# Recurrent mixer scan: the products of the states with r move from VectorE to GpSimd, and some small VectorE operands move to PSUM

## What is computed

```python
def step(state, rkv):
    r_t, k_t, v_t = rkv
    pred = jnp.einsum('bhij,bhj->bhi', state, k_t)
    err = pred - v_t
    state = dec * state - et * (err[..., :, None] * k_t[..., None, :])
    n = jnp.maximum(jnp.sqrt(jnp.sum(state * state, axis=(-2, -1), keepdims=True)), 1e-08)
    state = state * jnp.where(n > max_norm, max_norm / n, 1.0)
    wkv = jnp.einsum('bhij,bhj->bhi', state, r_t)
    return (state, wkv)
```

## Time and profile before

| | |
|---|---|
| median of 3 runs | 7446.54 us (7446.42 to 7454.33) |
| the profiled execution: its own time | 7440.85 us |
| the profiled execution: its span | 7439.0 us |
| stage `mixer_scan`, in the span | 230 to 1349 us |
| VectorE busy in that stage | 1063.57 of 1119 us |
| GpSimd busy in that stage | 0 us |

### The profile page before, as it was taken

How to read it: one execution, slowest core, us unless ns; L and a number is a source line. 1 busy time by engine, 2 the same in 40 slices (tenths; PEclk the granted TensorE clock), 3 DMA queues, 4 the chain that set the end, 5 groups by cost and what they waited for, 6 DMA issues and landing times. The chain is left out here.

```text
span 7439.0 us, 185174 instructions
## 1 busy us (share of the span) xinstructions
PE 6202.7 (83%) x76196; PEld 4530.6 (61%) x76196; DVE 5784.1 (78%) x10537; ACT 3453.0 (46%) x7490; POOL 3111.7 (42%) x1651
## 2 busy tenths in 40 slices
PE   6455555599996789999999999997878699999999
PEld 4445554477775655555555555554555488888888
DVE  8899999555546769999999999997565477777775
ACT  4333333233332367777777777774444311111111
POOL 1000000111110049999999999997122122222222
PEclk8767777799998899999999999998889799999999
DMA  3211111201102330211202112111111100000000
GB/s 99 62 38 47 45 40 37 67 31 41 39 14 85 119 102 20 63 39 40 56 28 57 37 40 56 40 39 40 39 50 41 74 6 7 8 7 8 8 7 6
DMA packets 385855, 312.95 MB, mean 42 GB/s; under 512 B 169443, under 2 KB 354790, under 8 KB 384646
## 3 DMA queue, kind: packets, MB, share of 16 engines
q1 hardware_dynamic: 382566, 300.75, 13.8%
q10 hardware_dynamic: 2464, 0.26, 0.0%
HBM read 193.93 MB, written 106.95 MB: 40 GB/s over the span
## 5 line engine op out<-in xcount | busy, mean ns | idle before, releaser
L1865 POOL TENSOR_TENSOR ss_ch<-ss_h,ss_c_all 128x1024 f32<-128x1024 f32 x1024 | 2401.1, 2395 | 161.3 <-DVE ss_h L1888 126.4
L1888 DVE TENSOR_TENSOR_SCAN ss_h<-ss_decay,banks 128x1024 f32<-128x1024 f32 x1024 | 2259.8, 2268 | 169.1 <-PE banks L1785 164.6
L1785 PE MATMUL banks<-ss_diag,ss_dxT 128*32 128x256 f32 x32768 | 1985.3, 383 | 85.8 <-ACT ss_diag L1835 71.7
L1785 PEld LDWEIGHTS banks<-ss_diag,ss_dxT 128*32 128x32 f32 x32768 | 1003.0, 110 | 895.6 <-DVE ss_h L1888 263.1
L1844 ACT ACTIVATE ss_decay<-ss_dt,ss_neg_a 128x510 f32<-128x510 f32 x2048 | 1359.9, 711 | 299.0 <-DVE ss_h L1888 292.8
L627 PE MATMUL banks<-ms_rprod,ident 128*128 128x128 f32 x2048 | 466.9, 400 | 509.6 <-DVE ms_rprod L713 509.6
L2190 POOL TENSOR_TENSOR pk_blockhot<-pk_onehot,pk_parts 128x2048 bf16<-128x2048 bf16 x96 | 345.4, 3626 | 1100.0 <-DVE pk_parts L2428 1100.0
L1835 ACT ACTIVATE ss_diag<-ident,ss_bT 128x128 f32<-128x128 f32 x2048 | 694.9, 387 | 224.5 <-PE banks L1785 215.1
L627 PEld LDWEIGHTS banks<-ms_rprod,ident 128*128 128x128 f32 x2048 | 431.9, 263 | 539.4 <-DVE ms_rprod L713 475.7
L1792 PE MATMUL banks<-ss_ch,ss_stacked 128*32 128x256 f32 x8192 | 639.4, 383 | 80.1 <-POOL ss_ch L1865 80.1
L1047 DVE TENSOR_REDUCE l_nmax<-banks 128x2 f32<-128x512 f32 (+1 forms) x512 | 318.2, 621 | 342.4 <-PE banks L1032 340.8
(11 more groups left out here) (295 smaller groups left out, 9593.4 us busy)
## 6 DMA issues: line engine op xcount, KB each, us to landing
ss_c_all<-keep_cn SPq DMA_DIRECT2D x512, 64.0 KB, 2.1
ss_dt<-keep_dt SPq DMA_DIRECT2D x256, 128.0 KB, 3.6
keep_v<-ms_cx_values SPq DMA_DIRECT2D x32, 512.0 KB, 2.8
l_va<-keep_v SPq DMA_DIRECT2D x32, 512.0 KB, 5.3
l_kf<-keep_k SPq DMA_DIRECT2D x32, 256.0 KB, 3.2
keep_x<-l_x SPq DMA_DIRECT2D x32, 256.0 KB, 2.2
keep_xc<-si_xc SPq DMA_DIRECT2D x16, 512.0 KB, 3.9
keep_zs<-si_zs SPq DMA_DIRECT2D x16, 512.0 KB, 4.9
```

The lines of the kernel that those rows point to most:

```text
L1785: m = T_.matmul(inp[u % 2][s * CB:(s + 1) * CB, g, :, t * P:(t + 1) * P], inputs[i % 2][0][:, g, t, u * CB:(u + 1) * CB], diag[slot][:, g, ...
L1865: G_.tensor_tensor(whole(ch[u % CHS]), whole(h[u % 4]), whole(c_all[slot]), ALU.mult).then_inc(weighed, 1)
L1888: V.tensor_tensor_scan(whole(h[u % 4]), whole(decay[u % 4]), whole(inp[u % 2]), 0.0, ALU.mult, ALU.add).then_inc(scanned, 1)
```

## The change

The change has three parts.

First, `rprod` is made by GpSimd, in a new function `gpsimd(G)`, one instruction for each of the 256 tokens. For token n it waits for the mark `multiplied` of step n + 1, which is `prod` of the next step (the instruction that reads the same state), so it starts when that one ends. Because two engines now read a state, VectorE waits in step t, ahead of the new state, until GpSimd has made the product of token t - 2, which reads the buffer that is written over. TensorE's wait for a group is adapted to a mark on every product.

Second, on VectorE the order in a step is new: `prod`, at once `raw`, and only then `inv` and `FF`.

Third, `raw` and `pred` lie in bank 7 of PSUM, and so does a copy of the decay, `dec_held`, made once. So `pred`, `fdec` and `err` have one input in PSUM and one in SBUF, where they had two in SBUF. `inv` and the reciprocal keep their one input, and their output, in SBUF. `prod`, `outer` and the new state keep two inputs in SBUF.

```diff
-    raw, pred, err = sb("raw", [P, 2 * D]), sb("pred", [P, 2 * D]), sb("err", [P, 2, D])
+    err = sb("err", [P, 2, D])
+    raw, pred, dec_held = bank[7][:, 128:128 + 2 * D], bank[7][:, 192:192 + 2 * D], bank[7][:, 256:258]
...
-                T_.wait_ge(*multiplied_r.at(q))
+                T_.wait_ge(*multiplied_r.at((q + 1) * GR - 1))
...
+        V.tensor_copy(dec_held, dec[:, :]).then_inc(*own.up())
...
-        V.wait_ge(*state.at(T - 1))
-        r_product(V, T)
...
+    def gpsimd(G):
+
+        for n in range(T):
+            if n % CH == 0:
+                G.wait_ge(*steps[n // CH % 2].at(n // CH // 2))
+            if n >= 2 * GR and n % GR == 0:
+                G.wait_ge(*summed_r.at(n // GR - 2))
+            if n < T - 1:
+                G.wait_ge(*multiplied.at(n + 1))
+            else:
+                G.wait_ge(*state.at(n))
+            G.tensor_tensor(rprod[:, n // GR % 2, n % GR, :, :].rearrange("p (e i) j -> p e i j", e=2), S_[:, (n + 1) % 2, :, :, :],
+                            rep(R_[:, n, :, :], 2, D), ALU.mult).then_inc(multiplied_r.sem, 1)
...
-        V.tensor_tensor(prod[:, :, :, :], now, rep(K_[:, t, :, :], 2, D), ALU.mult).then_inc(*own.up())
-        multiplied = own.now()
+        V.tensor_tensor(prod[:, :, :, :], now, rep(K_[:, t, :, :], 2, D), ALU.mult).then_inc(multiplied.sem, 1)
+        V.wait_ge(*multiplied.at(t))
+        V.tensor_reduce(raw, prod[:, :, :, :].rearrange("p e i j -> p (e i) j"), AX.X, ALU.add).then_inc(*own.up())
         if t:
-            r_product(V, t)
             V.wait_ge(*rooted.at(t - 1))
             V.tensor_scalar(inv[:, :], root[:, :], 1.0 / max_norm, 1.0, ALU.mult, ALU.max).then_inc(*own.up())
-        inverted = own.now()
-        V.wait_ge(*multiplied)
-        V.tensor_reduce(raw[:, :], prod[:, :, :, :].rearrange("p e i j -> p (e i) j"), AX.X, ALU.add).then_inc(*own.up())
-        if t:
-            V.wait_ge(*inverted)
+            V.wait_ge(*own.now())
             V.reciprocal(FF[:, t, :], inv[:, :]).then_inc(*own.up())
...
+        if t > 1:
+            V.wait_ge(*multiplied_r.at(t - 2))
...
+    gpsimd(nc.gpsimd)
     vector(nc.vector)
```

More of the change, by code:

```diff
@@ L574, in mixer_scan @@
     half, state, rooted = st.mark("first_head_ready"), st.mark("state"), st.mark("rooted")
-    squared, multiplied_r, summed_r, cut = st.mark("squared", 2), st.mark("r_multiplied"), st.mark("r_summed"), st.mark("r_cut")
+    squared, multiplied, multiplied_r, summed_r, cut = st.mark("squared", 2), st.mark("multiplied"), st.mark("r_multiplied"), st.mark("r_summed"), st.mark("r_cut")
     measured, spread_root, spread_ready = st.mark("measured"), st.mark("spread_root"), st.mark("spread_ready")
@@ L733, in step @@
             V.wait_ge(*state.at(t - 1))
-        V.tensor_tensor(prod[:, :, :, :], now, rep(K_[:, t, :, :], 2, D), ALU.mult).then_inc(*own.up())
-        multiplied = own.now()
+        V.tensor_tensor(prod[:, :, :, :], now, rep(K_[:, t, :, :], 2, D), ALU.mult).then_inc(multiplied.sem, 1)
+        V.wait_ge(*multiplied.at(t))
+        V.tensor_reduce(raw, prod[:, :, :, :].rearrange("p e i j -> p (e i) j"), AX.X, ALU.add).then_inc(*own.up())
         if t:
-            r_product(V, t)
             V.wait_ge(*rooted.at(t - 1))
             V.tensor_scalar(inv[:, :], root[:, :], 1.0 / max_norm, 1.0, ALU.mult, ALU.max).then_inc(*own.up())
-        inverted = own.now()
-        V.wait_ge(*multiplied)
-        V.tensor_reduce(raw[:, :], prod[:, :, :, :].rearrange("p e i j -> p (e i) j"), AX.X, ALU.add).then_inc(*own.up())
-        if t:
-            V.wait_ge(*inverted)
+            V.wait_ge(*own.now())
             V.reciprocal(FF[:, t, :], inv[:, :]).then_inc(*own.up())
         V.wait_ge(*own.now())
-        V.tensor_tensor(by_e(pred[:, :]), by_e(raw[:, :]), rep(FF[:, t, :], 2, D), ALU.mult).then_inc(*own.up())
+        V.tensor_tensor(by_e(pred), by_e(raw), rep(FF[:, t, :], 2, D), ALU.mult).then_inc(*own.up())
         predicted = own.now()
-        V.tensor_tensor(fdec[:, :], FF[:, t, :], dec[:, :], ALU.mult).then_inc(*own.up())
+        V.tensor_tensor(fdec[:, :], FF[:, t, :], dec_held, ALU.mult).then_inc(*own.up())
         V.wait_ge(*predicted)
-        V.tensor_tensor(err[:, :, :].rearrange("p e i -> p (e i)"), pred[:, :], VV[:, t, :, :].rearrange("p e i -> p (e i)"),
+        V.tensor_tensor(err[:, :, :].rearrange("p e i -> p (e i)"), pred, VV[:, t, :, :].rearrange("p e i -> p (e i)"),
                         ALU.subtract).then_inc(*own.up())
```

## The result

The changed kernel takes 7515.03 us (median of 4 runs, 7512.84 to 7516.7) against 7450.43 us for the kernel before, timed beside it: a ratio of 1.0085, 95% interval 1.0067 to 1.0102. The forecast was 7512.

What follows compares the result with a forecast made beforehand. VectorE's chain of instructions bounds the edited stage, busy 1063.57 of 1119.00 us. The step, 3.81 + 0.60 = 4.41 against 4.15 us, costs 66 us, plus 1: 7512 us; range 7350 to 7545, 8 times in 10.

Steps and rivals of the forecast that it cites:

- `prod` to `raw` 0.73: VectorE's step: `raw` starts 0.73 us after `prod`, as nothing stands between them any more.
- `raw` to `inv` 0.60: VectorE's step: `inv` starts 0.60 us after `raw`, at 1.33, with the root there since 0.88.
- from `FF` on the old distances: VectorE's step: from `FF` to the next `prod` the order and the distances between starts stay as before.
- The sum without any hold, 3.81: One step added up from starts in rows: 3.81 us, 0.34 less than 4.15, 87 us gained over 255 steps.
- rival B: `inv` of two numbers runs in the plain form, nothing is held: step 3.81, time 7361 us; chance 0.21.
- GpSimd's product: In each step it starts at 0.78 us, 0.09 after `prod` ends, and takes 1.30 (bounds 1.16 to 1.44).
- `inv` held, `FF` late by 0.60: `inv` ends with GpSimd's product, at 2.09 instead of 1.49 us; `FF` starts at 2.13 instead of 1.53.
- the indirect sign, 9 ns more: With a wait, TENSOR_SCALAR and CAST of 2 numbers take 169 ns, a two-input instruction 160: taken as sign of the fast form.
- The step 4.41: 3.81 + 0.60 us with `inv` held, 0.26 longer than before: 66 us over 255 steps, plus 1 us of small terms.
- `pred`, `fdec` and `err` free by their PSUM operands: Beside GpSimd's product these VectorE instructions, with one input in PSUM, cost nothing more.
- `outer` clear of the product: GpSimd has long finished when `outer` starts; without a hold GpSimd ends at 2.08 us and `outer` starts at 2.17.
- Rival C: `inv` is free but the reciprocal is held, or a hold is partly covered: step 4.22, time 7465 us; chance 0.06.

Runs made afterwards that it cites:

- e3_small_sbuf: The changed kernel with `inv` written to PSUM, and `raw`, `pred` and the decay back in SBUF: 7416.93 us, ratio 0.9949.
- e1_root_psum: The changed kernel with the input of `inv` (`root`) in PSUM and its output still in SBUF: 7367.48 us, ratio 0.9886.
- e6_one_number: The changed kernel with `inv` made by two instructions of one number each, all operands still in SBUF: 7377.67 us, ratio 0.9897.
- e5_two_products: The changed kernel with GpSimd's product in two instructions of 256 numbers, `inv` still in SBUF: 7386.51 us, ratio 0.9914.
- e8_fused_err: The changed kernel with `inv` written to PSUM, and `pred` and `err` made by two scalar_tensor_tensor instructions: 7359.52 us, ratio 0.9878.

## Why the prediction was right, step by step

- `prod` to `raw` 0.73, `raw` to `inv` 0.60, from `FF` on the old distances: in the profile after they are 0.72, 0.60, and 2.30 from `FF` to the next `prod` (forecast 2.28).
- The sum without any hold, 3.81: shown by the kernel with `inv` written to PSUM. Its rows give 3.82 (1199.61 + 3.82 = 1203.43, the next `raw`), and its time, 7370, is the 7361 of rival B within 9 us. Some 3 of the 9 are a step that the sum left out: in the twelfth step of each chunk the root isn't there at 0.88, because ScalarE has a copy to make first, and that step takes 4.01.
- GpSimd's product: release 0.09 after `prod` (measured 0.08 in the step shown), length 1.30 taken from the fixed part and the slope of other rows (measured 1.266; the bounds were 1.16 and 1.44).
- `inv` held, `FF` late by 0.60: measured `inv` 0.73 instead of 0.16, so 0.57. It was the step that decided the sign and the one that no row showed directly; the indirect sign, 9 ns more for the kinds with a fast form, pointed the right way. It was a thin one: it rests on single rows of 2 numbers, and the reciprocal, which isn't held, takes 165 ns behind a wait in the same trace, 4 less than `inv`.
- The step 4.41 (measured 4.39), the loss 66 + 1 us: measured 65 on the medians. That the two meet this closely is partly luck. The product was 0.03 shorter than forecast and the usual step 0.02, which leaves 255 x 0.24 = 61 us. And the wait of GpSimd for a free `rprod` buffer, which I had put at nothing, goes with 62 steps that are some 0.09 longer, 6 us.
- `pred`, `fdec` and `err` free by their PSUM operands: 0.20, 0.15 and 0.19 beside the product, and 47 us lost without them (e3_small_sbuf).
- `outer` clear of the product: it starts at 2.75 of the step. Rival B had it at 2.17 with 0.09 to spare and no cost even if touched; with `inv` free it stayed at 0.69.
- Rival C, the reciprocal held: fallen; from SBUF to SBUF it is 0.17 long in the middle of a product (e1_root_psum and e6_one_number).

What the change was worth is thus a sum of two: the product on GpSimd and the new order with all small instructions free, -82 us, and `inv` held, +145 us (7515 - 7370). No run separates the product on GpSimd from the new order; how the 82 divide between them stays an estimate of the sum.

## What to carry to other kernels

When work goes to GpSimd beside VectorE, go through every VectorE instruction that starts in that stretch, also those of two numbers. Held here were those with two inputs in SBUF (`pred` with 32 numbers, `outer` with 512) and two with one input and output in SBUF, a cast of 512 numbers and a tensor_scalar of two. One operand in PSUM freed `inv` and `pred`, input or output for `inv`, at no cost that the times can tell. A cast or a copy with an operand in PSUM, and odd counts above one, weren't run. The price of a hold isn't the size of the held instruction but what is left of GpSimd's, and all that waits behind. If no operand can be moved, cutting GpSimd's instruction in two got most of it back here (e5_two_products, 7387 us), since the hold ends with the instruction under way; that holds where the VectorE instruction comes while the first half is running.

## What the runs showed that I had not expected

- One number per instruction isn't held: `inv` in two instructions of one number takes 137 us less than in one instruction of two, and the median is 7 us over that of the PSUM version (e6_one_number).
- A scalar that VectorE reads from SBUF (`FF` in e8_fused_err), beside one input in SBUF and one in PSUM, isn't held. All 512 of them take 0.22 to 0.24 us, those beside the product and those of the first step, which has no product beside it. In the step shown the first starts 0.31 before the end of the product and is done 0.08 before it.
- GpSimd starts a product some 0.07 later where it has also waited for a free buffer, although that had long been free: 62 steps, 6 us of the change's 65.
